# Holding back the second half of two indirect scatters in a mixture-of-experts and scan kernel

## The chip, the cores and the metric

The kernel runs on one core of a Trainium2 chip. The metric is the device time of one execution in microseconds; each kernel is run several times and the median counts. The engines are TensorE (PE, with its weight loads as PEld), VectorE (DVE), ScalarE (ACT), GpSimd (POOL) and SyncE (SP), which only issues DMAs. They run side by side and are tied together by semaphores.

## The reference, cut to what matters

The input is x of 32 x 256 tokens with 128 features. Three blocks follow one another, each on a layer-normed input and added to the residual; the first and the last are the same feed-forward block with the same weights.

```python
def ffn(x, Wr, br, W1, b1, W2, b2):              # 16 experts, 128 -> 256 -> 128
    probs = softmax(x @ Wr + br)
    w, idx = top_k(probs, 2); w = w / sum(w)
    comb = zeros(T, 16).at[arange(T)[:, None], idx].add(w)
    h = gelu(einsum('td,edh->teh', x, W1) + b1)  # exact gelu
    o = einsum('teh,eho->teo', h, W2) + b2
    return x + einsum('teo,te->to', o, comb)

def attn(x, gamma, wq, wk, wv, wa, wg, wo):
    xn = rms_norm(x) * gamma
    q, k, v, a, g = xn @ wq, xn @ wk, xn @ wv, xn @ wa, xn @ wg
    a = complex(*split(a)); a = sigmoid(abs(a)) * exp(1j * angle(a))
    y = real(associative_scan(y[t] = a[t] * y[t-1] + k[t] * v[t]))   # along the sequence
    return (q * y * silu(g)) @ wo

x = x + 0.5 * ffn(layernorm(x)); x = x + attn(layernorm(x)); x = x + 0.5 * ffn(layernorm(x))
```

## The kernel before, in words

The tokens are cut into four groups (g = 0 to 3) of 2048, 16 tiles of 128 tokens each, and every group stays in SBUF as X[:, g]. The feed-forward block is done twice (f = 0 and f = 1). The kernel computes only the chosen experts: the router's result is turned into a row number for each of a token's two choices, the normed rows are scattered to DRAM sorted by expert, the experts run over tiles of 128 sorted rows, and their results are gathered back and added.

One hand-written list, ORDER, gives the order of all steps, and each engine walks it and does its own part of every step. The steps that matter here:

- R(f, g), K(f, g): router logits on TensorE; VectorE picks the two experts, ranks the rows and writes the row numbers IDX (L1039).
- P(f, g): POOL's scatter. Its first half is 16 indirect DMAs of one tile each (L466), for every token's first choice. The second half (L474) is 16 more for the second choice. Before each eight of these POOL waits until eight of the first half have landed and copies the second weight into the rows' last column (L471). Every indirect DMA is issued by POOL and moves 128 rows.
- E(f, g, half, lo, hi): experts over the pairs of tiles from lo to hi. SP loads the sorted rows (xs, L366) and the experts' weights (WUP, L360), four tiles' rows at a time. Before the first rows of a group it waits until that group's scatter has landed. TensorE transposes the rows (L776), multiplies by the up weights (L786) and the down weights (L803); ScalarE moves what lies between out of PSUM (xsT L551, hidT L532, eo L540) and issues the stores to rows_out (L546). A group has 24 pairs. The pairs are counted through the kernel by the semaphore eo_sb.
- G(f, g, lo, hi): POOL's gather (L487), quarters lo to hi of a group, 8 indirect DMAs for a quarter.
- C(f, g, lo, hi): VectorE adds the gathered rows to X (L1069, L1070).
- N, S, T, A0, A, I, H, A1, J, AP, U, A2, A3 (g): the middle block for a group. T: transposes (L837), A0 and A: 24 products on TensorE (L863), counted through the kernel by the semaphore proj_ps (1 to 24 for group 0, 25 to 48 for group 1, 49 to 72 for group 2, 73 to 96 for group 3); then long VectorE operations on 128x2048 tiles, ScalarE's functions and a scan; A3: the output projection (L875, 16 products in four banks), which VectorE adds to X bank by bank (L1139).

The groups are staggered: while the middle block of one group runs its scan, the experts of the one before and the one after it fill TensorE. POOL's own order around the change is P(1,0), G(0,3), P(1,1), G(1,0), P(1,2), G(1,1). On TensorE the order is: last experts of (0,2); A3 of group 1; the last four pairs of (0,3); T and A of group 2; experts 0 to 8 of (1,0); 8 to 20 of (1,0); A3 of group 2; and the same again one group later.

So that POOL's DMAs don't all come at once, each of them can be held back. Two tables give, for every DMA of every P and G step, the number of expert pairs (PAIRS_BY) and of attention products (PRODUCTS_BY) that must have been made:

```python
def keep_behind(st, i):
    if i % 1 == 0 and PAIRS_BY[st][i // 1] > waited[0]:
        waited[0] = PAIRS_BY[st][i // 1]
        pool.wait_ge(eo_sb, waited[0])
    if i % 1 == 0 and PRODUCTS_BY[st][i // 1] > waited[1]:
        waited[1] = PRODUCTS_BY[st][i // 1]
        pool.wait_ge(proj_ps, waited[1])
```

A wait that was made once isn't made again. A P step has 32 entries, the first 16 for its first half. In P(1,0) the pairs' table ends at 95, in P(1,1) at 119.

Of the kernel before, what the change touches and what calls it, by code (L numbers as in the profile page):

```python
# [16 lines left out]
P = 128  # L17
# [86 lines left out]
               ("P", 0, 3, 0): (20, 20, 20, 20, 20, 20, 20, 20, 20, 20, 20, 20, 20, 20, 20, 20, 20, 20, 20, 20, 20, 20, 21, 23, 24, 26, 27, 29, 30, 32, 33, 34),  # L104
               ("G", 0, 2, 0, 3): (36, 38, 39, 41, 42, 44, 44, 44, 44, 44, 44, 44, 44, 44, 44, 44, 44, 44, 44, 44, 44, 44, 44, 44),
               ("G", 0, 2, 3, 4): (44, 44, 44, 44, 44, 44, 44, 44),
               ("P", 1, 0, 0): (44, 44, 44, 44, 44, 44, 44, 44, 44, 44, 44, 44, 44, 44, 44, 44, 44, 44, 44, 44, 44, 44, 44, 44, 44, 44, 44, 44, 44, 44, 46, 47),
               ("G", 0, 3, 0, 2): (49, 50, 52, 53, 55, 56, 58, 59, 61, 62, 63, 65, 66, 68, 68, 68),
               ("G", 0, 3, 2, 3): (68, 68, 68, 68, 68, 68, 68, 68), ("G", 0, 3, 3, 4): (68, 68, 68, 68, 68, 68, 68, 68),
               ("P", 1, 1, 0): (68, 68, 68, 68, 68, 68, 68, 68, 68, 68, 68, 68, 68, 68, 68, 68, 68, 68, 68, 68, 68, 68, 68, 68, 68, 68, 68, 68, 68, 68, 70, 71),  # L110
               ("G", 1, 0, 0, 4): (73, 74, 76, 77, 79, 80, 82, 83, 85, 86, 88, 89, 91, 92, 92, 92, 92, 92, 92, 92, 92, 92, 92, 92, 92, 92, 92, 92, 92, 92, 92, 92),
               ("P", 1, 2, 0): (92, 92, 92, 92, 92, 92, 92, 92, 92, 92, 92, 92, 92, 92, 92, 92, 92, 92, 92, 92, 92, 92, 92, 92, 92, 92, 92, 92, 92, 92, 92, 92),
               ("G", 1, 1, 0, 1): (92, 92, 92, 92, 92, 92, 92, 92), ("G", 1, 1, 1, 2): (92, 92, 92, 92, 92, 92, 92, 92),
# [1077 lines left out]
```

## Time and profile before

| | |
|---|---|
| median of 3 runs | 983.22 us (975.99 to 983.95) |
| span of the profiled execution | 994.3 us |
| TensorE matmul busy | 725.1 us, 73% |
| VectorE busy | 546.3 us, 55% |
| ScalarE busy | 514.7 us, 52% |
| GpSimd busy | 590.6 us, 59% |
| mean granted TensorE clock | 0.858 of full |
| DMA | 167.13 MB, 168 GB/s over the span |

A profiled execution is one execution on the chip, recorded instruction by instruction; its span runs from the first to the last instruction, and all times below count from its start. Busy time is the time in which an engine had an instruction under way; a matmul's end is modelled, so the moment at which another engine gets its result can be later than the recorded end.

### The profile page before, as it was taken

How to read it: one execution, taken by the hardware profiler on the slowest of the kernel's cores; microseconds unless marked ns; L12 is line 12 of the kernel's file. 1: busy time of each engine (PE TensorE's matmuls, PEld its weight loads, DVE VectorE, ACT ScalarE, POOL GpSimd, SP SyncE). 2: the span in 40 equal slices, each digit the busy share in tenths (PEclk: the TensorE clock that was granted, in tenths of full speed). 3: DMA queues.
4: the chain of work that ended last, by engine and by line, in shares of the span. 5: the costliest groups of instructions: out<-in, count | busy, mean ns of one | idle time of the engine just before them, and what ended most of it. 6: DMA issues, size and time to landing. Idle time of an engine off the chain costs nothing.

```text
span 994.3 us, 15862 instructions
## 1 busy us (share of the span) xinstructions
PE 725.1 (73%) x4409; PEld 607.2 (61%) x4410; DVE 546.3 (55%) x1352; ACT 514.7 (52%) x1071; POOL 590.6 (59%) x551
## 2 busy tenths in 40 slices
PE   4775888786876888669777967685968648977761
PEld 4234788685366873469644867534958627777650
DVE  7983103106689955799745996647876455010201
ACT  1111556455777637676277773576664315444340
POOL 2277441555777747758467457378657545655555
PEclk9995899889977989789788779795989759999986
DMA  9995587774146833176441456321758517778863
GB/s 327 299 348 165 149 234 228 208 202 130 40 123 195 224 111 105 42 202 194 121 124 46 129 161 202 99 66 40 217 167 250 141 41 199 221 207 226 234 201 103
DMA packets 188846, 167.13 MB, mean 168 GB/s; under 512 B 18976, under 2 KB 176480, under 8 KB 187744
## 3 DMA queue, kind: packets, MB, share of 16 engines
q1 hardware_dynamic: 120736, 106.83, 36.6%
q0 software_dynamic: 16384, 33.72, 11.5%
q10 hardware_dynamic: 51648, 25.63, 8.8%
q8 instruction: 39, 0.64, 0.3%
q14 instruction: 39, 0.32, 0.1%
HBM read 104.57 MB, written 61.51 MB: 167 GB/s over the span
## 4 chain that ended last, share of the span: by engine, by line
PE 48%; issue 12%; ACT 12%; another core or an unknown queue 9%; SPq 7%; DVE 5%; DMA 5%; ACTq 0%; DVEq 0%
PE bank L786 17%; PE bank L803 16%; PE bank L863 7%; DMA WUP<-up_weights 4%; PE bank L776 4%; ACT eo L540 2%; SPq L319 2%; PE bank L758 2%; SPq L360 1%; SPq L330 1%; ACT hidT L532 1%; PE bank L702 1%; ACT ci L623 1%; ACT xsT L551 1%
## 5 line engine op out<-in xcount | busy, mean ns | idle before, releaser
L487 POOL DMA_INDIRECT got<-rows_out,IDX x256 | 285.8, 1117 | 194.2 <-ACT eo L540 86.5
L786 PE MATMUL bank<-xsT,WUP 128*128 128x128 f32 x1564 | 240.0, 303 | 77.4 <-ACT xsT L551 51.1
L786 PEld LDWEIGHTS bank<-xsT,WUP 128*128 128x128 f32 x1564 | 218.8, 216 | 85.9 <-issue 75.2
L803 PE MATMUL bank<-W,hidT 128*128 x1564 | 221.0, 286 | 41.5 <-ACT hidT L532 32.1
L803 PEld LDWEIGHTS bank<-W,hidT 128*128 128x128 f32 x1564 | 199.3, 199 | 51.4 <-issue 49.6
L466 POOL DMA_INDIRECT rows_in<-XL,IDX x128 | 157.1, 1227 | 109.3 <-DVE IDX L1039 46.5
L474 POOL DMA_INDIRECT rows_in<-XL,IDX x128 | 136.3, 1065 | 91.7 <-ACT eo L540 53.7
L540 ACT ACTIVATE eo<-bank,xs 128x128 f32<-128x128 f32 x391 | 122.7, 367 | 109.9 <-PE bank L803 74.6
L532 ACT ACTIVATE hidT<-bank 128x512 f32<-128x512 f32 x200 | 118.1, 591 | 116.1 <-PE bank L786 72.8
L551 ACT ACTIVATE xsT<-bank 128x256 f32<-128x256 f32 x200 | 74.0, 377 | 86.2 <-remote 39.2
L863 PE MATMUL bank<-XT,WA 128*128 128x512 f32 x192 | 94.6, 654 | 21.2 <-DVE qg L1090 10.4
L776 PE MATMUL bank<-ident,xs 128*128 128x128 f32 x391 | 81.8, 301 | 5.7 <-issue 3.1
L1069 DVE TENSOR_TENSOR X<-got,X 128x512 f32<-128x512 f32 x32 | 22.0, 686 | 116.3 <-DMA got<-rows_out,IDX 102.2
L863 PEld LDWEIGHTS bank<-XT,WA 128*128 128x128 f32 x192 | 39.1, 207 | 72.8 <-issue 57.6
L1062 DVE TENSOR_TENSOR X<-bank,X 128x512 f32<-128x512 f32 x32 | 21.3, 687 | 96.5 <-issue 41.4
L776 PEld LDWEIGHTS bank<-ident,xs 128*128 128x128 f32 x391 | 56.4, 161 | 8.5 <-issue 8.2
L712 PE MATMUL bank<-WR,hidT 128*128 128x16 f32 x192 | 38.9, 341 | 21.9 <-issue 20.9
L712 PEld LDWEIGHTS bank<-WR,hidT 128*128 128x128 f32 x192 | 38.5, 297 | 23.9 <-issue 23.8
L758 PE MATMUL bank<-B,CT 128*128 128x512 f32 x64 | 37.0, 708 | 15.8 <-issue 9.0
L913 DVE BATCH_NORM_STATS2 stats<-X 128x6 f32<-128x128 f32 x192 | 38.3, 278 | 6.0 <-DMA X<-in_L_attn_x 5.8
L1011 DVE TENSOR_SCALAR den<-gexp 128x16 f32<-128x16 f32 x8 | 1.4, 173 | 62.0 <-ACT gexp L516 60.8
L969 DVE TENSOR_SCALAR XL<-X,rs,nb 128x128 f32<-128x128 f32 x128 | 33.8, 360 | 1.0 <-DVE rs L951 0.8
(150 smaller groups left out, 900.4 us busy)
## 6 DMA issues: line engine op xcount, KB each, us to landing
WUP<-up_weights SPq DMA_DIRECT2D x400, 128.0 KB
xs<-rows_in SPq DMA_DIRECT2D x100, 258.0 KB
rows_out<-eo ACTq DMA_DIRECT2D x91, 256.0 KB
rows_in<-kv SPq DMA_DIRECT2D x16, 774.0 KB, 12.1
X<-in_L_attn_x SPq DMA_DIRECT2D x4, 1024.0 KB, 7.7
rows_in<-XL,IDX POOLq DMA_INDIRECT x256
got<-rows_out,IDX POOLq DMA_INDIRECT x256
out<-X SPq DMA_DIRECT2D x4, 1024.0 KB
```

The lines of the kernel that those rows point to most:

```text
L466: pool.indirect_dma_start(rows_in[slot], bass.IndirectOffsetOnAxis(IDX[:, g, j, 0:1], 0), XL[:, b, j, :], None).then_inc(first_put[i], 16)
L474: pool.indirect_dma_start(rows_in[slot], bass.IndirectOffsetOnAxis(IDX[:, g, j, 1:2], 0), XL[:, b, j, :], None).then_inc(scattered[which], 16)
L487: pool.indirect_dma_start(got[:, k, j, :], None, rows_out[SLOT[f, g, half]][0:rows, :], bass.IndirectOffsetOnAxis(IDX[:, g, j, k:k + 1], 0 ...
L532: act.activation(hidT[:, v, 0:tiles * 2 * P], ps[2 + v][:, 0:tiles * 2 * P], ACT.Gelu).then_inc(hid_sb, 1)
L540: ins = act.activation(eo[:, u // 2, t, :], ps[6 + u % 2][:, a * D:(a + 1) * D], ACT.Copy, scale=xs[:, buf, t, D:D + 1])
L551: act.activation(xsT[:, v, 0:tiles * P], ps[v][:, 0:tiles * P], ACT.Copy).then_inc(xsT_sb, 1)
L712: ins = pe.matmul(ps[4][:, j * E:(j + 1) * E], rowsT[i - 1][:, j % 4 * P:(j % 4 + 1) * P], WR[:], start=True, stop=True)
L758: pe.matmul(ps[5 - i][:], CT[:, half * P:(half + 1) * P], B2[:, i, :], start=True, stop=True).then_inc(bias_ps, 1)
L776: ins = pe.transpose(ps[u % 2][:, a * P:(a + 1) * P], xs[:, buf, u % 2 * 2 + a, 0:D], ident[:])
L786: ins = pe.matmul(ps[2 + u % 2][:, k * P:(k + 1) * P], WUP[:, u, a, c * P:(c + 1) * P], xsT[:, u % 2, a * P:(a + 1) * P], start=True, stop ...
L803: ins = pe.matmul(o, hidT[:, v, (2 * a + c) * P:(2 * a + c + 1) * P], W2[:, ds(e * H + c * D, D)], start=(c == 0), stop=(c == 1))
L863: pe.matmul(ps[turns_of[k % 6]][:], WA[:, w, :], XT[:, blk * 512:(blk + 1) * 512], start=True, stop=True).then_inc(proj_ps, 1)
```

## The change

Two rows of PRODUCTS_BY are changed, those of P(1,0) and P(1,1). In each, the second 16 entries are set to the number of the first product of the next group's attention, 49 (group 2) and 73 (group 3). The first 16 entries stay; the two entries of 46 and 47 (70 and 71), which the counts have passed when the scatter starts, go away. Nothing else is changed: the same DMAs in the same order, on the same queue.

```diff
-               ("P", 1, 0, 0): (44, 44, 44, 44, 44, 44, 44, 44, 44, 44, 44, 44, 44, 44, 44, 44, 44, 44, 44, 44, 44, 44, 44, 44, 44, 44, 44, 44, 44, 44, 46, 47),
+               ("P", 1, 0, 0): (44, 44, 44, 44, 44, 44, 44, 44, 44, 44, 44, 44, 44, 44, 44, 44, 49, 49, 49, 49, 49, 49, 49, 49, 49, 49, 49, 49, 49, 49, 49, 49),
                ("G", 0, 3, 0, 2): (49, 50, 52, 53, 55, 56, 58, 59, 61, 62, 63, 65, 66, 68, 68, 68),
                ("G", 0, 3, 2, 3): (68, 68, 68, 68, 68, 68, 68, 68), ("G", 0, 3, 3, 4): (68, 68, 68, 68, 68, 68, 68, 68),
-               ("P", 1, 1, 0): (68, 68, 68, 68, 68, 68, 68, 68, 68, 68, 68, 68, 68, 68, 68, 68, 68, 68, 68, 68, 68, 68, 68, 68, 68, 68, 68, 68, 68, 68, 70, 71),
+               ("P", 1, 1, 0): (68, 68, 68, 68, 68, 68, 68, 68, 68, 68, 68, 68, 68, 68, 68, 68, 73, 73, 73, 73, 73, 73, 73, 73, 73, 73, 73, 73, 73, 73, 73, 73),
                ("G", 1, 0, 0, 4): (73, 74, 76, 77, 79, 80, 82, 83, 85, 86, 88, 89, 91, 92, 92, 92, 92, 92, 92, 92, 92, 92, 92, 92, 92, 92, 92, 92, 92, 92, 92, 92),
```

## Rows read from the trace of the kernel before

**Rows 1.** The page: busy time by engine, and the chain's shares by engine and by line.

```profile
PE 725.1 (73%) x4409; PEld 607.2 (61%) x4410; DVE 546.3 (55%) x1352; ACT 514.7 (52%) x1071; POOL 590.6 (59%) x551
...
PE 48%; issue 12%; ACT 12%; another core or an unknown queue 9%; SPq 7%; DVE 5%; DMA 5%; ACTq 0%; DVEq 0%
...
PE bank L786 17%; PE bank L803 16%; PE bank L863 7%; DMA WUP<-up_weights 4%; PE bank L776 4%; ACT eo L540 2%; SPq L319 2%; PE bank L758 2%; SPq L360 1%; SPq L330 1%; ACT hidT L532 1%; PE bank L702 1%; ACT ci L623 1%; ACT xsT L551 1%
```

**Rows 2.** POOL's timeline around P(1,0)'s second half: start, us, line, output and input, idle before it.

```profile
477.93 0.98 POOL L474 DMA_INDIRECT rows_in<-XL,IDX  x1 [0.28 <-issue]
...
486.79 0.96 POOL L474 DMA_INDIRECT rows_in<-XL,IDX  x1 [0.30 <-issue]
...
507.06 0.96 POOL L474 DMA_INDIRECT rows_in<-XL,IDX  x1 [0.30 <-issue]
...
511.16 0.97 POOL L487 DMA_INDIRECT got<-rows_out,IDX  x1 [3.15 <-PE bank L863]
```

**Rows 3.** POOL's timeline at G(1,0)'s start.

```profile
646.19 0.98 POOL L487 DMA_INDIRECT got<-rows_out,IDX  x1 [5.72 <-PE bank L863]
```

**Rows 4.** SP's timeline, loads of sorted rows; several issues are merged.

```profile
509.46 1.48 SPq L366 DMA_DIRECT2D xs<-rows_in  x3
...
641.86 1.48 SPq L366 DMA_DIRECT2D xs<-rows_in  x3
...
762.61 1.25 SPq L366 DMA_DIRECT2D xs<-rows_in  x2
```

**Rows 5.** The chain in order of time: start, us, what.

```profile
89.36 3.08 DMA xs<-rows_in
...
784.59 16.80 another core or an unknown queue
```

**Rows 6.** TensorE's timeline: output projections and first transposes of rows.

```profile
475.88 7.26 PE L875 MATMUL bank<-WO,kv 128*128 128x128 f32 x32 [0.71 <-issue]
...
550.29 1.09 PE L776 MATMUL bank<-ident,xs 128*128 128x128 f32 x4
...
692.88 1.06 PE L776 MATMUL bank<-ident,xs 128*128 128x128 f32 x4
...
761.15 7.23 PE L875 MATMUL bank<-WO,kv 128*128 128x128 f32 x32 [1.28 <-issue]
...
768.22 0.60 PE L776 MATMUL bank<-ident,xs 128*128 128x128 f32 x4
```

**Rows 7.** VectorE's timeline: last projection bank of groups 1 to 3, additions of gathered rows.

```profile
488.24 0.69 DVE L1139 TENSOR_TENSOR X<-bank,X 128x512 f32<-128x512 f32 x1 [3.55 <-remote]
...
571.08 0.68 DVE L1069 TENSOR_TENSOR X<-got,X 128x512 f32<-128x512 f32 x1
...
622.45 0.69 DVE L1139 TENSOR_TENSOR X<-bank,X 128x512 f32<-128x512 f32 x1 [3.57 <-remote]
...
728.00 0.69 DVE L1069 TENSOR_TENSOR X<-got,X 128x512 f32<-128x512 f32 x1
...
768.42 0.69 DVE L1139 TENSOR_TENSOR X<-bank,X 128x512 f32<-128x512 f32 x1 [1.06 <-issue]
```

**Rows 8.** POOL's timeline in G(0,3) and at P(1,1)'s start.

```profile
542.81 2.57 POOL L487 DMA_INDIRECT got<-rows_out,IDX  x1 [0.30 <-issue]
...
580.19 1.45 POOL L466 DMA_INDIRECT rows_in<-XL,IDX  x1 [11.24 <-DVE IDX L1039]
```

**Rows 9.** POOL's timeline in P(1,2).

```profile
700.45 1.00 POOL L466 DMA_INDIRECT rows_in<-XL,IDX  x1 [3.78 <-ACT eo L540]
...
738.97 1.03 POOL L474 DMA_INDIRECT rows_in<-XL,IDX  x1 [6.06 <-ACT eo L540]
...
744.99 1.42 POOL L474 DMA_INDIRECT rows_in<-XL,IDX  x1 [0.91 <-ACT eo L540]
...
760.23 0.96 POOL L474 DMA_INDIRECT rows_in<-XL,IDX  x1 [0.30 <-issue]
```

**Rows 10.** A stretch: length, busy us of each engine (instructions), granted clock, DMA share, GB/s.

```profile
553.00:580.00 27.00, 18.83 (x146) 18.23 (x146) 25.83 (x49) 20.83 (x39) 7.19 (x6) 0.82 0.62 173
```

## The prediction

> **What bounds the kernel now.** I read the page first: TensorE is the busiest engine and holds nearly half of the chain that ended last, GpSimd (POOL) is busy 59% of the span and has no line of its own in that chain [rows 1]. So POOL costs time only where somebody waits for one of its DMAs. The change moves 2 x 16 of them, so the second view is POOL's timeline around the two scatters, to be read for two things: when the second half (L474) runs today, and what POOL does behind it. In the first scatter, P(1,0), the second half starts at 477.93, straight behind the first half; its last DMA starts at 507.06. Then POOL waits until 511.16, where the product count reaches 49, for the first gather of group 3 [rows 2]. In P(1,1) the pattern is the same: behind its last scatter POOL waits 5.72 us, until 646.19, for count 73 [rows 3]. Third, the readers of what POOL delivers: SP's loads of rows (L366), TensorE's first transposes on them (L776), VectorE's additions of gathered rows (L1069) and the indices that start the next scatter [rows 4 to 8].
>
> **Where the scatters go.** 49 and 73 are the counts for which the first gather behind each scatter waits already. So I take the start from those gathers: the second halves begin at 511.16 and 646.19. Eight undisturbed scatters have their first and last starts 8.86 us apart, 1.266 us each [rows 2]; 16 of them and the weight copies between take 16 x 1.266 + 0.5 = 20.7 us. What is queued behind them on POOL goes back by 20.7 us: 32 gathers of group 3, then P(1,1); 32 gathers of group 0, then P(1,2), then the gathers of group 1. No DMA is added or taken away, and the wait is one that POOL would make a few lines later.
>
> **First site, cover by cover.** (a) SP waits for the scatter before it loads the first rows of the next experts, at 509.46 today, 1.4 us after the last scatter ended (507.06 + 0.96). It would load at 511.16 + 20.7 + 1.4 = 533.3; a load of rows shows 3.08 us in the chain [rows 5], so they are there at 536.4, and TensorE asks at 550.29: 13.9 us of cover [rows 4, 6]. Behind that load SP has only the next rows and the weights of the same stage. Cost 0. (b) The first 16 gathers of group 3 would run from 531.9. Undisturbed, one takes 0.94 + 0.30 = 1.24 us. A gather at 542.81 took 2.57 us, and its next three some 2 us, while VectorE was in operations on whole 128x2048 tiles [rows 8]; with 4.7 us for those four, the 16 are done at 557, plus 2 for landing. VectorE adds them at 571.08 [rows 7]: 12 us of cover. The other 16 end near 580, and their additions come after the next scan, some 30 us behind the first ones. Cost 0. (c) P(1,1) starts at 580.19, when its indices are written, and POOL idled 11.24 us before it [rows 8]. Laid end to end, 32 x 1.24 + 4.7 and 3 more for other held ones from 531.9 give 579.3: just in time. A few us late would not matter, since that scatter's second half now waits till 646 anyway. Cost 0.
>
> A rule bears on the held DMAs. The gather at 542.81 is held beside VectorE operations with two SBUF inputs. The Trainium skill, SBUF — State Buffer, "Who interferes with whom", says that such an operation takes only a read interface and, as an inference, leaves descriptor generation alone. This trace does not agree; by the rule the 4.7 us would be 0 and the second site below would end some 3 us earlier, at a cost of 0. The sum stays with the rows.
>
> **Second site.** (a) SP's load at 641.86 goes to 646.19 + 20.7 + 1.4 and some 2 us for held scatters = 670, rows there at 673; TensorE takes them at 692.88 [rows 4, 6]: 19 us. (b) Gathers of group 0 would run from 669. Before, they ran from 646.19 to 696.67 (700.45 less the wait of 3.78) [rows 3, 9], 50.5 us; with the same holds they end at about 719 and have landed by 721. VectorE adds them from 728.00 [rows 7]: 7 us of cover. (c) P(1,2) started at 700.45 and would start at 719. From here the slack is thin. From 646.19 to its end at 761.19 (760.23 + 0.96) POOL waited for pair counts six times, from the 3.78 us at 700.45 to 0.91 us at 744.99, the longest 6.06 us at 738.97, in all 13.6 us, 11.8 us beyond the 0.3 us that every DMA has anyway [rows 9]. So the end can move by 20.7 - 11.8 = 8.9 us at most if everything else stays, and by 0 at least. Laid out: first 16 to 739.3 (16 x 1.266), four more and the copy to 745, then 12 x 1.266 + 0.5 + four held by 1.06 = 19.9, end 764.9: 3.7 us later. (d) This one has a near reader: SP waited for it and loaded at 762.61; with 3.1 us the rows are there at 765.7, TensorE takes them at 768.22 [rows 4, 6], a slack of 2.5 us. So the cost is 3.7 - 2.5 = 1.2 us, between 0 and 8.9 - 2.5 = 6.4. I count it as on the path in full: the pairs that read these rows stand in TensorE's queue ahead of the last group's router.
>
> **DMA traffic.** In 553 to 580 five gathers ran beside eight pairs of experts at a DMA share of 0.62 [rows 10]; now there would be some 19. Waits for expert weights make 4% of the chain [rows 1], 40 us over 200 pairs, 0.2 us a pair; were they doubled for these eight pairs, that is 1.6 us. Between 0 and 1.6; I take 0.3, since the share is far from full. In 478 to 508 traffic falls, and TensorE's long wait there is not for a DMA. Gain 0.
>
> Sum: +1.2 + 0.3 = +1.5 us on a span of 994.3. The three timed runs lie at 976 to 984, so the profiled execution is some 11 us longer; a term of 1.5 us carries over as it is: 983.2 + 1.5 = 984.7, with 983.2 to 991.2 as this case's own range (0 to 6.4 + 1.6).
>
> **Rival 1, the scatters hold TensorE up today.** After the attention of groups 1 and 2 the output projection's 32 matmuls (L875) are issued in 7.26 us, from 475.88 in group 1 [rows 6], which ends at 483.14, yet VectorE gets the last bank at 488.24, 5.1 us later, after a wait of 3.55 us; in group 2 it waits 3.57 us, until 622.45 [rows 7]. Scatters of exactly the moved half run beside. The same matmuls in group 3, from 761.15 for 7.23 us with gathers beside them, hand over at 768.42, at once [rows 6, 7]. The next norm waits for that bank, so about 5.1 us lie on the path, twice. If the scatters do it, the gain is 10.2 us less the 1.5: 974.5. Against it: group 3's gathers are DMAs of the same queue and do no harm there, and 16.80 us of waiting that the chain can't name stand at 784.59, beside gathers alone [rows 5]. If half of it comes back elsewhere, the gain is 3 to 4 us.
> The Trainium skill, SBUF — State Buffer, "Who interferes with whom", states that TensorE and ScalarE never wait on anyone and that a DMA never contends with a compute engine; by it this rival brings nothing and the time is the forecast's. The late hand-over is then something that the change leaves.
>
> **Rival 2, POOL's backlog reaches the path.** The 20.7 us go into a stretch in which POOL catches up only by its waits. It decides once P(1,2)'s last scatter ends after 761.2 + 2.5 = 763.7. If the pair counts come at the same times, the price is at most 6.4; if more DMAs are held by VectorE (1.06 us each), it nears the full 20.7 - 2.5 = 18.2. The middle of the two and 0.3 for traffic gives 12: 995. For it: POOL is idle little in 664 to 761; against it: 6.06 us of waiting in one piece [rows 9].
>
> **Rival 3, it moves nothing.** The waits could be met already, or the covers take all: 983.2. The rows deny the first (count 49 lets POOL go at 511, not at 478) [rows 2]; the second is the forecast's lower end.
>
> **How the numbers follow.** Forecast case 0.57; rival 1 0.26 (974.5, from 970 to 980); rival 2 0.12 (995); nothing at all 0.05. What a measurement of this kernel can tell from no change is about 1%, 9.8 us: 973.4 and 993.0. Faster by over 1%: 0.20, most of rival 1, whose full size stands on that line and which the runs' own spread of 0.8% can carry over it; slower by over 1%: 0.11, nearly all of rival 2; within 1%: 0.69. Range 972 to 991: the forecast's own, and most of rival 1; rival 2 is left out.
>
> **What would show it.** POOL idle from 477.9 to 511 and from about 610 to 646, the second halves as one run of about 21 us behind the first products; SP's loads near 533 and 670; TensorE's transposes at 550 and 693 unmoved; POOL without its 11 us pause before 580; P(1,2)'s end at 762 to 768, SP's load 1.4 us behind. Rival 1 shows in the last L1139 of groups 1 and 2: right behind L875 if true, still 5 us late if not. I am wrong if these hand-overs close up, if TensorE waits for P(1,2)'s rows by more than 6 us, or if its transposes (L776) wait for rows at 550 or 693.

## The result and the profile after

The changed kernel takes 988.95 us (median of 15 runs, 982.27 to 1006.25), the kernel before 977.99 us beside it (15 runs, 971.54 to 990.59). The ratio is 1.0136, 95% interval 1.0110 to 1.0162: slower by 1.4%, some 13 us. The forecast was +1.5 us.

The two profiled executions don't show this as a total: 992.0 us after, 994.3 us before. Single executions differ by more than the effect, so they have to be read stretch by stretch. The page of the kernel after:

```profile
PE 730.7 (74%) x4409; PEld 607.1 (61%) x4410; DVE 546.3 (55%) x1352; ACT 515.0 (52%) x1071; POOL 600.1 (60%) x551
...
PE 49%; ACT 13%; issue 12%; DVE 8%; another core or an unknown queue 6%; DMA 5%; SPq 4%; POOL 1%; ACTq 0%; POOLq 0%; DVEq 0%
...
L803 PE MATMUL bank<-W,hidT 128*128 x1564 | 225.6, 289 | 46.8 <-issue 30.7
```

POOL has taken hardly anything of the chain (1%), and nothing in the busy times stands out. The row of L803, the down products of the experts, counts 46.8 us in which TensorE was idle just before one of them (41.5 in the kernel before); it matters below. POOL's timeline answers to [rows 2, 3, 9]:

```profile
505.60 0.98 POOL L474 DMA_INDIRECT rows_in<-XL,IDX  x1 [27.08 <-PE bank L863]
...
529.22 0.98 POOL L487 DMA_INDIRECT got<-rows_out,IDX  x1 [0.30 <-issue]
...
580.12 4.57 POOL L466 DMA_INDIRECT rows_in<-XL,IDX  x1 [0.30 <-issue]
...
636.85 0.98 POOL L474 DMA_INDIRECT rows_in<-XL,IDX  x1 [26.88 <-PE bank L863]
...
661.03 0.98 POOL L487 DMA_INDIRECT got<-rows_out,IDX  x1 [0.30 <-issue]
...
713.07 1.00 POOL L466 DMA_INDIRECT rows_in<-XL,IDX  x1 [0.30 <-issue]
...
727.05 0.96 POOL L466 DMA_INDIRECT rows_in<-XL,IDX  x1 [0.30 <-issue]
...
767.13 0.96 POOL L474 DMA_INDIRECT rows_in<-XL,IDX  x1 [0.30 <-issue]
```

The waits do what they say: POOL is idle for 27.08 us until the first product of group 2 and for 26.88 us until that of group 3. The second halves take 23.6 us (505.60 to 529.22) and 24.2 us (636.85 to 661.03). P(1,1) starts straight behind the last gather (580.12, idle 0.30), and from 636.85 to 728.0 POOL has no pause longer than 1.07 us. P(1,2) starts at 713.07 and ends at 767.13 + 0.96 = 768.1. The readers and the marks of TensorE's course, in answer to [rows 4, 6, 7]:

```profile
530.62 1.49 SPq L366 DMA_DIRECT2D xs<-rows_in  x3
...
662.26 1.48 SPq L366 DMA_DIRECT2D xs<-rows_in  x3
...
769.57 1.29 SPq L366 DMA_DIRECT2D xs<-rows_in  x2
```

```profile
479.63 7.26 PE L875 MATMUL bank<-WO,kv 128*128 128x128 f32 x32 [2.53 <-ACT eo L540]
502.79 9.18 PE L863 MATMUL bank<-XT,WA 128*128 128x512 f32 x14 [2.24 <-ACT XT L582]
...
545.47 1.09 PE L776 MATMUL bank<-ident,xs 128*128 128x128 f32 x4
...
611.47 7.25 PE L875 MATMUL bank<-WO,kv 128*128 128x128 f32 x32 [4.68 <-ACT eo L540]
634.52 9.23 PE L863 MATMUL bank<-XT,WA 128*128 128x512 f32 x17 [2.90 <-ACT XT L582]
...
683.74 1.06 PE L776 MATMUL bank<-ident,xs 128*128 128x128 f32 x4
...
768.16 7.23 PE L875 MATMUL bank<-WO,kv 128*128 128x128 f32 x32 [1.29 <-issue]
775.23 0.60 PE L776 MATMUL bank<-ident,xs 128*128 128x128 f32 x4
```

```profile
486.93 0.69 DVE L1139 TENSOR_TENSOR X<-bank,X 128x512 f32<-128x512 f32 x1 [1.06 <-PE bank L875]
...
618.76 0.69 DVE L1139 TENSOR_TENSOR X<-bank,X 128x512 f32<-128x512 f32 x1 [1.06 <-PE bank L875]
```

No transpose (L776) waits for rows: at 545.47, 683.74 and 775.23 there is no idle time ahead of them. And the last bank of the output projection is taken by VectorE (L1139) at 486.93 and 618.76, within 0.1 us of the end of L875 (479.63 + 7.26, 611.47 + 7.25). The late hand-over of 5.1 us in groups 1 and 2 [rows 6, 7] is gone, which was the sign for rival 1. The first product then follows at 502.79 and 634.52. In the kernel before it came later behind the same matmuls:

```profile
508.31 9.43 PE L863 MATMUL bank<-XT,WA 128*128 128x512 f32 x16 [2.88 <-issue]
...
643.33 9.32 PE L863 MATMUL bank<-XT,WA 128*128 128x512 f32 x14 [5.02 <-ACT XT L582]
```

From the end of L875 to the first product of the next group that is 25.2 and 26.0 us before, 15.9 and 15.8 us after: 19.5 us won. They are lost again further on. In the last pairs before the second half of experts (1,1) the trace has TensorE idle for 12.95 us:

```profile
711.50 1.06 PE L786 MATMUL bank<-xsT,WUP 128*128 128x128 f32 x8
714.54 1.15 PE L803 MATMUL bank<-W,hidT 128*128 x8 [1.99 <-issue]
728.65 2.07 PE L803 MATMUL bank<-W,hidT 128*128 x8 [12.95 <-issue]
```

```profile
727.85 0.60 ACT L532 ACTIVATE hidT<-bank 128x512 f32<-128x512 f32 x1 [9.18 <-remote]
```

The trace puts the 12.95 us ahead of the eight matmuls L803 at 728.65 down to "issue", to nothing that it knows, but the order of events says more. These matmuls follow ScalarE's hidT at once (727.85 + 0.60 = 728.45), and ScalarE waited for the last up products, L786, whose recorded end is 711.50 + 1.06 = 712.56: it got them 15.3 us later. Nothing that these up products needed is shown as missing. This is what "stand-still" means below: a result of matmuls already issued reaches the next engine many us late, and TensorE has nothing else to do meanwhile. Whether TensorE works late or only its signal is late, the trace doesn't tell, since matmul ends are modelled. The stand-still lies beside the first twelve scatters of P(1,2), which run without a break from 713.07 to 728.01.

### The profile page after: what moved, and what is told of

The parts are those of the page before. It is cut to its first block, busy times and chain, and to the rows that moved or that the text cites. A ratio compares the mean times of both kernels' runs of the same rounds, so it can differ in the third digit from the quotient of the medians.

```text
span 992.0 us, 15862 instructions
## 1 busy us (share of the span) xinstructions
PE 730.7 (74%) x4409; PEld 607.1 (61%) x4410; DVE 546.3 (55%) x1352; ACT 515.0 (52%) x1071; POOL 600.1 (60%) x551
## 4 chain that ended last, share of the span: by engine, by line
PE 49%; ACT 13%; issue 12%; DVE 8%; another core or an unknown queue 6%; DMA 5%; SPq 4%; POOL 1%; ACTq 0%; POOLq 0%; DVEq 0%
PE bank L786 15%; PE bank L803 13%; PE bank L863 8%; DMA WUP<-up_weights 5%; PE bank L776 4%; PE bank L875 3%; PE bank L712 3%; SPq L360 3%; ACT eo L540 2%; PE bank L758 2%; PE bank L702 2%; ACT hidT L532 1%; ACT kv L502 1%; ACT XT L582 1%
## 5 line engine op out<-in xcount | busy, mean ns | idle before, releaser
L487 POOL DMA_INDIRECT got<-rows_out,IDX x256 | 292.9, 1144 | 159.8 <-issue 74.7
L786 PE MATMUL bank<-xsT,WUP 128*128 128x128 f32 x1564 | 233.4, 297 | 59.8 <-ACT xsT L551 37.6
L803 PE MATMUL bank<-W,hidT 128*128 x1564 | 225.6, 289 | 46.8 <-issue 30.7
L786 PEld LDWEIGHTS bank<-xsT,WUP 128*128 128x128 f32 x1564 | 212.3, 210 | 68.4 <-issue 53.9
L803 PEld LDWEIGHTS bank<-W,hidT 128*128 128x128 f32 x1564 | 201.9, 201 | 60.1 <-issue 57.6
L532 ACT ACTIVATE hidT<-bank 128x512 f32<-128x512 f32 x200 | 118.2, 591 | 117.9 <-PE bank L786 57.3
L863 PE MATMUL bank<-XT,WA 128*128 128x512 f32 x192 | 94.7, 654 | 18.5 <-ACT XT L582 8.0
L776 PE MATMUL bank<-ident,xs 128*128 128x128 f32 x391 | 82.0, 301 | 3.7 <-DMA xs<-rows_in 1.9
L863 PEld LDWEIGHTS bank<-XT,WA 128*128 128x128 f32 x192 | 39.2, 208 | 70.3 <-issue 58.7
L1062 DVE TENSOR_TENSOR X<-bank,X 128x512 f32<-128x512 f32 x32 | 21.3, 687 | 103.8 <-PE bank L758 94.7
L776 PEld LDWEIGHTS bank<-ident,xs 128*128 128x128 f32 x391 | 55.2, 160 | 6.4 <-issue 5.7
L875 PE MATMUL bank<-WO,kv 128*128 128x128 f32 x128 | 29.0, 399 | 14.5 <-issue 7.3
L875 PEld LDWEIGHTS bank<-WO,kv 128*128 128x128 f32 x128 | 28.3, 311 | 15.3 <-issue 7.7
## 6 DMA issues: line engine op xcount, KB each, us to landing
rows_in<-kv SPq DMA_DIRECT2D x16, 774.0 KB, 12.4
```

Source lines behind the costliest of these rows:

```text
L487: pool.indirect_dma_start(got[:, k, j, :], None, rows_out[SLOT[f, g, half]][0:rows, :], bass.IndirectOffsetOnAxis(IDX[:, g, j, k:k + 1], 0 ...
L532: act.activation(hidT[:, v, 0:tiles * 2 * P], ps[2 + v][:, 0:tiles * 2 * P], ACT.Gelu).then_inc(hid_sb, 1)
L776: ins = pe.transpose(ps[u % 2][:, a * P:(a + 1) * P], xs[:, buf, u % 2 * 2 + a, 0:D], ident[:])
L786: ins = pe.matmul(ps[2 + u % 2][:, k * P:(k + 1) * P], WUP[:, u, a, c * P:(c + 1) * P], xsT[:, u % 2, a * P:(a + 1) * P], start=True, stop ...
L803: ins = pe.matmul(o, hidT[:, v, (2 * a + c) * P:(2 * a + c + 1) * P], W2[:, ds(e * H + c * D, D)], start=(c == 0), stop=(c == 1))
L863: pe.matmul(ps[turns_of[k % 6]][:], WA[:, w, :], XT[:, blk * 512:(blk + 1) * 512], start=True, stop=True).then_inc(proj_ps, 1)
```

## Four stretches that can be compared

I cut every execution at the same marks: the ends of the three output projections (start plus duration of L875) and the first product of groups 2 and 3 (first L863 behind it). The runs were made in six series, each on one chip. They are of two kinds, told apart by what the kernel before takes in them: 978 to 997 us in four (called slow chips here, the first result's series among them; the record doesn't name its chip), 880 and 883 us in two (quick chips). None of the five chips that are named was used twice, so that the chip makes the difference, and not the hour, is likely but not shown. "Held" are kernels in which both second halves wait for 49 and 73; kernels in which the second half of P(1,0) or P(1,1) waits for something else are not in the table. "A3(1) to 49" is the passage from the end of group 1's output projection to product 49, and so on; "rest" runs from A3(3) to the end. The time ahead of the first mark is left out.

| us | kernel | A3(1) to 49 | 49 to A3(2) | A3(2) to 73 | 73 to A3(3) | rest |
|---|---|---|---|---|---|---|
| slow | before | 25.2 | 109.0 | 26.0 | 125.0 | 225.9 |
| slow | after | 15.9 | 115.9 | 15.8 | 140.9 | 216.6 |
| slow | after again (h4) | 15.9 | 116.0 | 15.8 | 140.3 | 216.4 |
| slow | before, readers late (g2) | 23.2 | 110.8 | 24.7 | 122.3 | 234.8 |
| slow | after, readers late (g1) | 15.9 | 114.6 | 15.8 | 142.3 | 235.2 |
| slow | before, half gather (h1, k2) | 21.4, 16.7 | 108.3, 107.7 | 23.3, 22.3 | 123.7, 122.8 | 212.8, 216.1 |
| slow | after, half gather (g4, k1) | 15.9, 15.9 | 117.1, 112.6 | 15.7, 15.8 | 121.5, 125.6 | 220.6, 221.2 |
| slow | after, repaced (h3) | 15.9 | 110.6 | 15.8 | 127.3 | 226.2 |
| quick | before (f1) | 15.9 | 107.6 | 15.7 | 120.0 | 176.8 |
| quick | after (f2) | 15.9 | 109.1 | 15.8 | 122.4 | 188.1 |

Each value is from one execution. The last column and the time ahead of the first mark vary from trace to trace without following the change: on slow chips, in the usual order of steps, the rest is 212.8 to 225.9 us where nothing is held and 216.4 to 226.2 where both are. So the columns don't add up to the measured ratios.

The experiments are told in the order in which they were made; S, B and C are the theories named in the expectations.

## Experiments: which site, and by how much

**Only the first site.** The diffs stand against the kernel before unless it is said otherwise, in PRODUCTS_BY unless another table is named; 44 x 16 is sixteen entries of 44.

```diff
-("P", 1, 0, 0): 44 x 30, 46, 47
+("P", 1, 0, 0): 44 x 16, 49 x 16
```

> Only P(1,0)'s second half waits for product 49; P(1,1) is as before. Theory S (the stream: POOL, robbed of its pauses, issues indirect DMAs without a break in the stretch around 712 to 728 of the changed kernel, and TensorE stands still beside it, 15.3 us there): the price belongs to the second site, where POOL is busy from 637 to 728 without a pause; the first site has an 11 us pause before P(1,1) as a buffer, so this kernel takes 978 +-4, a ratio of 0.995 to 1.004. Theory B (a backlog of POOL that delivers rows late, whichever site): the first site's readers have 12 us of cover and more, so also 1.00. Theory C (scatters or gathers beside attention and experts slow them, at each site alike): half of the 1.4%, 985, ratio 1.007.

Measured on a quick chip: 883.62 us against 882.65, ratio 0.9997 (0.9969 to 1.0024). The first site costs nothing there, as the prediction had it.

**Only the second site.**

```diff
-("P", 1, 1, 0): 68 x 30, 70, 71
+("P", 1, 1, 0): 68 x 16, 73 x 16
```

> Only P(1,1)'s second half waits for product 73; P(1,0) is as before. Theory S: nearly all of the loss, 985 to 992, ratio 1.010 to 1.016, with a stall of TensorE by more than 8 us in the twelve pairs of experts (1,1) beside an unbroken stream of POOL. Theory B: the same total, but TensorE waits for rows loaded behind P(1,2) (5 to 7 us near 768), not in the middle of experts (1,1). Theory C: half, 1.007.

896.49 us, ratio 1.0147 (1.0107 to 1.0187): the whole loss, on a chip on which the trace has no stand-still at all. TensorE waits 10.35 us at 717.37, for rows. That is theory B.

**Until the output projection is over.** Pair 93 and pair 117 are the first that TensorE makes behind A3.

In PAIRS_BY of the kernel before, the last sixteen entries:

```diff
-("P", 1, 0, 0): ..., 89, 90, 91, 91, 91, 91, 92, 92, 93, 94, 95 x 6
+("P", 1, 0, 0): ..., 93 x 9, 94, 95 x 6
-("P", 1, 1, 0): ..., 113, 114, 115, 115, 115, 115, 116, 116, 117, 118, 119 x 6
+("P", 1, 1, 0): ..., 117 x 9, 118, 119 x 6
```

> The second halves wait only until the output projection is over: for pair 93 (P(1,0)) and pair 117 (P(1,1)), near 492 and 623, some 14 us earlier than in the changed kernel, 14 us later than before. They end near 513 and 644, where they ended before within 6 us, so POOL keeps its later pauses. Theory S and B both: the loss of the changed kernel goes away, and if the hand-over of the output projection was held up by scatters (5.1 us late in two groups), there is a gain: 968 to 978, ratio 0.99 to 1.00. Theory C: scatters run beside attention as much as in the changed kernel, so it stays 0.5 to 1% slower than before.

885.12 us, ratio 1.0034 (1.0006 to 1.0062): a little over the range that S and B gave.

**P(1,2) without its pair counts.**

In PAIRS_BY of the kernel before:

```diff
-("P", 1, 2, 0): 121, 122, 122, 123, ..., 141, 142
+("P", 1, 2, 0): 120 x 32
```

> The kernel before with no pair count ahead of P(1,2)'s scatters: the scatters run in one stream from some 697 to 738, right behind the gathers of (1,0), and nothing is delivered later than before. Theory S: TensorE stalls beside this stream as in the changed kernel, 5 to 15 us: 983 to 992, ratio 1.005 to 1.015. Theory B: nothing is late, the rows are even earlier: ratio 0.995 to 1.002. Theory C has no more DMAs here than before, but closer together beside experts (1,1): up to 1.003.

882.41 us, ratio 0.9991 (0.9958 to 1.0023). An unbroken stream alone costs nothing on a quick chip. But the stream was not the quick one of some 40 us that I expected: P(1,2) starts at 637.61, once its indices are written, has no pause longer than 0.33 us, and still takes 56.1 us (to 693.76), while with its pair counts it takes 54.8 us in the kernel before on the other quick chip. Taking the waits away gave nothing back.

**Before and after on one quick chip.** Both are unchanged kernels.

> The kernel before, once more, for a trace from the same chip as the kernels beside it. In the runs on the quicker chip (before: 882.65) P(1,2)'s last scatter ended at 698.9 with only the first site changed, and TensorE took its rows at 706.8, right behind the last output projection. Theory B: the same here within 3 us, and no wait of TensorE ahead of those rows. Theory S: here too stand-stills of TensorE in the experts, beside long streams.

> The changed kernel, on the same chip as the others of this series. Theory B (POOL's backlog at the second site delivers P(1,2)'s rows late, the first site costs nothing): the ratio of the kernel with the second site alone, 1.0147 within 0.004, and in the trace P(1,2)'s last scatter some 14 us later than in the kernel before, TensorE's transposes of its rows some 10 us behind the last output projection. Theory S: the loss sits in stand-stills in the middle of experts, 5 us and more each. If both sites cost, more than 1.019.

The kernel after takes 895.34 us against 880.47, ratio 1.0161 (1.0133 to 1.0189). The kernel before, its timelines of TensorE and POOL:

```profile
557.76 7.26 PE L875 MATMUL bank<-WO,kv 128*128 128x128 f32 x32 [0.72 <-ACT eo L540]
580.74 9.23 PE L863 MATMUL bank<-XT,WA 128*128 128x512 f32 x17 [2.89 <-ACT XT L582]
...
693.47 7.23 PE L875 MATMUL bank<-WO,kv 128*128 128x128 f32 x32 [1.29 <-issue]
700.54 0.60 PE L776 MATMUL bank<-ident,xs 128*128 128x128 f32 x4
```

```profile
582.84 0.98 POOL L487 DMA_INDIRECT got<-rows_out,IDX  x1 [2.42 <-PE bank L863]
...
636.51 1.00 POOL L466 DMA_INDIRECT rows_in<-XL,IDX  x1 [4.56 <-ACT eo L540]
...
690.33 0.96 POOL L474 DMA_INDIRECT rows_in<-XL,IDX  x1 [0.30 <-issue]
```

And the kernel after:

```profile
698.24 7.22 PE L875 MATMUL bank<-WO,kv 128*128 128x128 f32 x32 [1.29 <-issue]
715.94 1.09 PE L776 MATMUL bank<-ident,xs 128*128 128x128 f32 x4 [10.47 <-DMA xs<-rows_in]
```

```profile
585.86 0.98 POOL L474 DMA_INDIRECT rows_in<-XL,IDX  x1 [18.69 <-PE bank L863]
...
609.09 0.97 POOL L487 DMA_INDIRECT got<-rows_out,IDX  x1 [0.31 <-issue]
...
660.82 1.00 POOL L466 DMA_INDIRECT rows_in<-XL,IDX  x1 [0.31 <-issue]
...
710.55 0.96 POOL L474 DMA_INDIRECT rows_in<-XL,IDX  x1 [0.30 <-issue]
```

The last row of TensorE is the price: the first transposes of P(1,2)'s rows wait 10.47 us for "DMA xs<-rows_in"; before they followed the output projection at once. From POOL's first DMA behind product 73 to the end of P(1,2) it is 108.5 us before (582.84 to 691.29) and 125.7 after (585.86 to 711.51), 17.2 us more. Of the second half's 23.2 us the gathers with the pause behind them (4.56 us at 636.51) gave back 1.9, since they ran slower than before, and P(1,2) itself 4.1 (54.8 us before, 50.7 after). Nothing else gave.

**Router first.** One edit of the changed kernel's order: R(1,3) ahead of the four pairs that read those rows.

```diff
-("A3", 3), ("E", 1, 2, 0, 0, 4), ("N", (1, 3), None), ("R", 1, 3), ("B", 1, 2, 0), ("K", 1, 3, 0),
+("A3", 3), ("N", (1, 3), None), ("R", 1, 3), ("E", 1, 2, 0, 0, 4), ("B", 1, 2, 0), ("K", 1, 3, 0),
```

> The changed kernel with the last group's norm and router, R(1,3), ahead of the four pairs of experts E(1,2,0,0,4) that read P(1,2)'s rows. The scatters come as late as before, but their first reader stands where TensorE would otherwise wait for the picks K(1,3). Theory B: the price goes away but for 0 to 3 us: ratio to before 0.998 to 1.004. Theory S, or contention of DMAs: the reader's place doesn't matter, and it stays at 1.012 to 1.017.

903.42 us, ratio 1.0235 (1.0201 to 1.0268): a miss, worse than the change itself. A reading of the order and the trace: the picks K(1,3) need a bias step on TensorE and an exponential on ScalarE, and both now stood behind the late pairs: VectorE's L1062 came at 738.95. The order had more readers than the one I moved, so this run doesn't judge theory B.

**Only the last eight.**

```diff
-("P", 1, 1, 0): 68 x 30, 70, 71
+("P", 1, 1, 0): 68 x 24, 73 x 8
```

> Only the last eight scatters of P(1,1) wait for product 73. They were held behind pair 117 already, some 15 us short of that. Theory B: the backlog is 10.4 us in place of 20.7, less the few us that they ran past the output projection before; the cushion ahead of TensorE is 3.4 us, so 2 to 6 us remain: ratio 1.002 to 1.007. Were the price set by whether anything is queued behind product 73, and not by how much, it would be as with all sixteen, 1.0147.

886.14 us, ratio 1.0057 (1.0035 to 1.0079), in the range of B. With it the quick chips give a row of doses. The third column is the end of P(1,2) less the end of L875 in group 3, the fourth TensorE's idle time ahead of L776:

| kernel | ratio | end of P(1,2) | wait |
|---|---|---|---|
| before (f1) | | -9.4 | none |
| first site only (e1) | 0.9997 | -8.1 | none |
| pairs 93 and 117 (e3) | 1.0034 | -3.3 | 1.08 |
| last eight (f4) | 1.0057 | -2.1 | 2.22 |
| second site only (e2) | 1.0147 | +6.0 | 10.35 |
| after (f2) | 1.0161 | +6.1 | 10.47 |

In all four that wait, it is the third column plus 4.3 to 4.4 us, the way from the last scatter over SP's load to the transpose. The cushion in the kernel before is 9.4 - 4.4 = 5 us. The wait is most of the loss: 10.5 of 14.2 us for the kernel after.

## Experiments: what else happens on a slow chip

**The readers late, after and before.** The four pairs stand behind all of K(1,3), once in the kernel after and once in the kernel before.

```diff
-("E", 1, 2, 0, 0, 4), ("N", (1, 3), None), ("R", 1, 3), ("B", 1, 2, 0), ("K", 1, 3, 0), ("K", 1, 3, 1),
+("N", (1, 3), None), ("R", 1, 3), ("B", 1, 2, 0), ("K", 1, 3, 0), ("K", 1, 3, 1), ("E", 1, 2, 0, 0, 4),
```

> The changed kernel with the four pairs E(1,2,0,0,4), the first readers of P(1,2)'s rows, behind the last group's norm, router and picks. Theory B: rows that come 10 us late are then early, since nobody asks for them before the picks; what remains is the price of the order itself, TensorE idle for 8.8 us during the norm: a ratio to before of 1.003 to 1.012, and the same time as the kernel before in this order (next kernel) within 0.4%. If something other than the lateness of these rows costs, the two differ by about 1.4% as the kernels themselves do.

> The kernel before in the same order, the control. Theory B: 1.003 to 1.012 of before, since the four pairs no longer fill TensorE's wait for the norm; the kernel above within 0.4% of it.

These fell on a slow chip (before: 995.75 us): ratio 1.0222 (1.0164 to 1.0281) after, 1.0154 (1.0102 to 1.0206) before. The order costs more than I gave it, and the difference of 0.7% lies between the two answers, the intervals overlapping. Inconclusive as a test of B; but the traces say why it had to be: on a slow chip A3(3) itself is late in the kernel after (142.3 us against 122.3), so the rows are not what is late.

**Held to product 85.** Against the kernel after:

```diff
-("P", 1, 1, 0): 68 x 16, 73 x 16
+("P", 1, 1, 0): 68 x 16, 85 x 16
```

> The changed kernel with P(1,1)'s second half held to product 85 in place of 73, 13 us later still; its own first reader has some 19 us left after the change and so stays covered. Theory B, with POOL full from the second half to the end of P(1,2): every us of delay goes through, P(1,2)'s last scatter comes 13 us later again, and the loss is 14 + 13 = 27 us: ratio 1.026 to 1.034. If POOL still had pauses to give, or the price were of another kind, it would stay at 1.015 to 1.02.

1016.25 us, ratio 1.0183 (1.0121 to 1.0245), less than expected and on a slow chip, on which the kernel after was not run as it is. The stretch from 73 to A3(3) is 153.9 us, 13 more than in the kernel after, so the delay went through there, with TensorE idle for 18.31 and 6.21 us ahead of the last two groups of L803 in that half of experts (735.36 and 743.64), the place of the stand-still above; the total is short of it by an amount that this run doesn't explain.

**Half a gather.** Against the kernel after, and for its control against the kernel before. The 16 gathers of group 0's second choice are left out, so its last addition uses old rows.

```diff
                     for k in range(2):
                         keep_behind(("G", f, g, lo, hi), 2 * j - lo * T // 2 + k)
+                        if (f, g, k) == (1, 0, 1):
+                            continue
...
-                    dve.wait_ge(got_in[q], 16 * 8 * (n + 1))
+                    dve.wait_ge(got_in[q], 16 * 8 * (n + 1) - (64 if n > 3 else 0))
```

> The changed kernel with both waits as they are, but G(1,0) gathers only each token's first choice; the 16 gathers of the second choice are left out, so group 0's last addition is of old rows. That takes some 16 x 1.3 = 21 us of work out of POOL's queue between the held scatters and P(1,2). Theory B: P(1,2) ends as early as before or earlier, and the loss goes: ratio 0.996 to 1.003. If the place of the held scatters costs (beside attention and experts) and not what is queued behind them, 1.010 to 1.016 stays.

981.95 us, ratio 0.9833 (0.9789 to 0.9878). Not only was the loss gone, the kernel was 1.7% faster than before, outside of what either theory gave. The next runs ask whether that was the hand-overs or the gathers.

> The control of the kernel with half of G(1,0): the kernel before, with the 16 gathers of group 0's second choice left out. Theory B alone: P(1,2) was early by some 3 to 5 us already, so 0.995 to 1.000, and the changed kernel without these gathers can be no better; that it was, 0.983 on a slow chip, then needs the late hand-overs of the output projection, which the held scatters take away (theory S: some 5 us twice). If this control is at 0.985 too, the gain came from the gathers left out.

978.06 us against 980.08, ratio 0.9987 (0.9951 to 1.0022), on another slow chip. Then both on one chip:

> The changed kernel with the 16 gathers of group 0's second choice left out, once more, now on the same chip as its control. Theory S, on a slow chip (kernel before above 970 us): the hand-overs of both output projections are prompt and POOL has its pauses back, so the kernel is 8 to 16 us faster than the control: 0.984 to 0.992 of before. Theory B alone, and on a quick chip (880 us): no backlog, nothing to win, 0.996 to 1.003, the same as the control within 0.4%.

> The control: the kernel before with the same 16 gathers left out. Measured once at 0.9987; again 0.995 to 1.002 on any chip. Were it below 0.99, leaving gathers out would itself be what made the other kernel faster.

Before: 997.44 us. With half a gather the changed kernel takes 983.60 us, ratio 0.9873 (0.9818 to 0.9929), the kernel before 996.96 us, ratio 0.9989 (0.9953 to 1.0026). So on a slow chip the same two waits are worth 1.2% of gain once POOL has the time for them, a gain known from the timed runs: the stretches of this one pair of traces don't show it (269.9 and 269.5 us over the first four), for k2 lost time ahead of the first mark. TensorE's timeline in the held one, k1 (here L877 is the output projection, L865 the products):

```profile
611.56 7.26 PE L877 MATMUL bank<-WO,kv 128*128 128x128 f32 x32 [0.72 <-ACT eo L542]
634.60 9.23 PE L865 MATMUL bank<-XT,WA 128*128 128x512 f32 x17 [2.88 <-ACT XT L584]
```

And in its control, k2:

```profile
624.34 7.26 PE L877 MATMUL bank<-WO,kv 128*128 128x128 f32 x32 [0.71 <-ACT eo L542]
653.91 9.23 PE L865 MATMUL bank<-XT,WA 128*128 128x512 f32 x17 [2.89 <-issue]
```

611.56 + 7.26 to 634.60 is 15.8 us; 624.34 + 7.26 to 653.91 is 22.3 us. At the first site k2's passage is only 16.7 us, but there TensorE was idle for 6.91 us ahead of the projection itself (499.91), beside the same scatters, and the first mark lies behind that.

**Pairs 93 and 117, on a slow chip.**

> The second halves wait for pair 93 and pair 117 only, once more, for a chip on which TensorE stands still beside streams of scatters. Theory S, on such a chip: the hand-overs after the output projection close up, 10 us less, and POOL is late by a few us only: ratio 0.985 to 0.998. On a chip without stand-stills 1.000 to 1.006, as measured there (1.0034).

986.99 us, ratio 1.0072 (1.0036 to 1.0109), where 0.985 to 0.998 was expected: a miss. The passages did close up (15.9 and 15.8 us), but the two stretches behind them took 118.2 and 133.4 us. The last four of group 2's products came only at 536.41, 32 us behind the first (25 us in the kernel after). SP's loads of rows and weights (516.35 to 522.80) now lie beside the products; whether they are the reason was not tried.

**Repaced.** Against the kernel after, in PAIRS_BY, the first entries; from the 21st on nothing changes:

```diff
-("P", 1, 2, 0): (121, 122, 122, 123, 124, 125, 126, 126, 127, 128, ...
+("P", 1, 2, 0): (129, 129, 130, 130, 131, 131, 132, 132, 132, 132, ...
```

> The changed kernel, with P(1,2)'s scatters tied to the pairs of experts that TensorE is making just then: two each behind pairs 129, 130, 131 and 132, the rest behind 132 at least. POOL then pauses as soon as TensorE falls behind. Theory S, on a chip with stand-stills: the one of 15 to 18 us in that stretch shrinks to 5 or less, and the ratio falls from 1.013 to 0.998 to 1.008, though the scatters end no earlier. Theory B: the pauses only delay POOL further: 1.013 to 1.02. On a chip without stand-stills the pairs are made before the scatters start and nothing changes, 1.014 to 1.017.

> The changed kernel beside the three above, on the same chip: 1.011 to 1.017, whichever chip it is. On a slow one with a stand-still of TensorE by 10 us or more in the first scatters of P(1,2), and prompt hand-overs after both output projections; on a quick one with P(1,2)'s rows late by 10 us.

984.24 us, ratio 1.0061 (1.0027 to 1.0094), and 987.40 us, ratio 1.0068 (1.0032 to 1.0104), on one slow chip. The kernel after shows its stand-still again, at the same eight matmuls and beside the same scatters:

```profile
724.70 2.07 PE L803 MATMUL bank<-W,hidT 128*128 x8 [10.17 <-issue]
```

In the repaced kernel it is absent, 73 to A3(3) took 127.3 us and not 140.3, but another came right behind. VectorE takes the last bank of A3(3), whose matmuls were issued from 745.99 for 7.23 us, only here:

```profile
767.21 0.69 DVE L1139 TENSOR_TENSOR X<-bank,X 128x512 f32<-128x512 f32 x1 [10.57 <-remote]
```

```profile
753.10 0.97 POOL L487 DMA_INDIRECT got<-rows_out,IDX  x1 [0.30 <-issue]
...
763.14 0.94 POOL L487 DMA_INDIRECT got<-rows_out,IDX  x1 [0.30 <-issue]
```

That is 14 us late, beside nine gathers in one stream from 753.10 to 764.08. Ahead of that, P(1,2) ended only 0.4 us before A3(3) and TensorE waited 3.90 us for its rows (at 757.13), the wait known from the quick chips. The net is nothing, 1.0061 against 1.0068. The edit was not the clean test that I meant: when the first scatter came, at 704.16, TensorE had only 16 down products of these pairs left (704.30 and 705.75), so it had hardly any experts in that stretch to stand still in, and no later scatter had to pause.

## Why the prediction was wrong, step by step

**What held.** The sign of the forecast, and that partly by luck: on the slow chips, where it was measured first, the loss is what is left of two larger effects, neither of which is in its sum. The waits act where I put them. At the first site SP loads at 530.62 (533.3 forecast), the transposes at 545.47 don't wait, P(1,1) starts just in time (580.12), and the site alone costs nothing on a quick chip. The additions of gathered rows had their cover.

**The step that failed: the end of P(1,2), +3.7 us.** I let POOL win back 17 of 20.7 us, 11.8 of them from its waits. Measured from its first DMA behind product 73 to the end of P(1,2): 115.0 us before and 131.2 after in the first pair of traces, 108.5 and 125.7 on a quick chip, so 16.2 and 17.2 us more. Three sizes were off. The second half took 23.2 to 24.2 us and not 20.7. P(1,2) took 50.7 (quick) or 55.0 us (slow) and not 45.9: on the quick chip without any waits, so its 32 scatters take 1.58 us each and not the 1.27 of undisturbed ones. And the waits were not slack to be had: with none of them P(1,2) took 56.1 us on a quick chip. The trace of the kernel before could have told: P(1,2) runs there from 700.45 to 761.19, and less the 8.3 us that its five waits for pair counts after the start last beyond 0.3 us each, that is 52.4 us. It has held DMAs, as the 2.57 us in [rows 8] is one; I priced four of them, at 1.06 us each.

**What it meant.** On the quick chips this is rival 2 as it stood: it decides once P(1,2) ends beyond the cushion, and its forecast was +12 us; measured 14.2, of which 10.5 are TensorE's wait for those rows. I gave it 0.12. "The end can move by 8.9 us at most" was the bound that ruled it out, and it was a sum of pauses, no bound.

**On the slow chips**, the result's own among them, nobody waits for those rows (only in the repaced kernel TensorE does, for 3.90 us): P(1,2) ends 7.2 us ahead of A3(3) before and 7.3 after, because the backlog went along with an A3(3) that is itself late. That path to the loss stands in no rival. And rival 1 was right as well (0.26), so the two pull against each other. The passage from A3 to the next product, behind groups 1 and 2, takes 15.7 to 15.9 us in every held trace on any chip and in every trace on a quick chip; on slow chips, with scatters beside the output projection, 16.7 to 26.0 us in eight passages, 22.9 on average. That is a gain of 7 us a passage, 14 in all. Against it stand 5.5 us in the stretch from 49 to A3(2) (114.5 on average in the five kernels with both waits and all gathers, 115.4 us in that held to 85 among them; 109.0 in the four not held) and 17.5 us from 73 to A3(3) (141.2 in three held, 123.7 in two not held). The sum is +9 us; measured +13 on the first chip, +7 on another. With half a gather the 17.5 go down to 0.3 and the sum to about -8; measured -12 (0.9873 less 0.9989, of 997). These sums are rough: they leave out the rest, where the held kernels with half a gather take 6 us more than their controls and the kernel after 9 us less than the one before. That the 17.5 us need the 16 gathers in POOL's queue is shown by four held and four not held traces, and by the ratios of the last pair. That they come by way of the stand-still is read from the traces, and there it is plain. Ahead of the last two groups of eight down products of experts 0 to 12 of (1,1), TensorE is idle for 14.9 us in the kernel after, 12.4 in h4, 16.4 with the readers late (g1) and 24.5 held to 85 (g3), where the stretch takes 17.2, 16.6, 18.6 and 30.2 us more than 123.7. In the other eight traces of slow chips, and in before and after on a quick one, it is at most 0.9 us. Up to 6 us of each stretch lie elsewhere.

**The term for DMA traffic**, +0.3 us, lies in the stretch from 49 to A3(2). It took 1.5 us more on the quick chip (109.1 and 107.6, one trace each) and 5.5 on slow chips. No run singles traffic out.

**Rival 3** was wrong: 49 and 73 moved everything they should.

**What stays open.** What makes TensorE stand still; what the 5.5 us of the first site are on a slow chip, since that site was tried alone on a quick one only; why pairs 93 and 117 lose on a slow chip what they gain. No version with the whole computation beat the kernel before by more than its interval. On a slow chip the gain of 1.2% is there for a kernel that takes 20 us out of POOL's queue between 637 and 713; no kernel here does so and still computes everything.

## What to carry to other kernels

The waiting time of an engine is not slack until it is shown that the instructions behind the wait run at their undisturbed speed: a count that looks late hides how slow they are. Follow a delayed queue to the first reader with a cushion smaller than the delay, and take the delay undiminished as the high end of the range. When a step is held away from a place where it hurts, ask what the queue does in the place where it now runs, and measure on more than one chip before believing a few tenths of a per cent.

## What was not expected of the hardware

The same program differs by 11 to 13% from one series, and chip, to another. The kernel before took 880.47 and 882.65 us in two and 977.99 to 997.44 us in four. The page shows where: idle time ahead of the down products, 46.8 us in the kernel after on a slow chip, above, and in its run on a quick one:

```profile
L803 PE MATMUL bank<-W,hidT 128*128 x1564 | 212.7, 279 | 3.5 <-ACT eo L540 1.2
```

On slow chips TensorE is idle for 5 to 18 us at a time with nothing missing that the trace knows. Three windows of the kernel after, with busy time and count of PE, PEld, DVE, ACT and POOL, then TensorE's granted clock, DMA share and GB/s:

```profile
705.00:712.00 7.00, 6.82 (x61) 6.63 (x61) 3.04 (x4) 4.06 (x12) 5.47 (x6) 1.00 0.87 247
712.00:728.00 16.00, 1.71 (x13) 1.33 (x12) 0.00 (x0) 1.56 (x5) 12.35 (x13) 0.65 0.44 133
728.00:731.00 3.00, 2.35 (x9) 2.21 (x10) 0.00 (x0) 0.71 (x2) 0.01 (x1) 0.50 0.68 180
```

The clock is full until the stand-still, 0.65 in it on average and 0.50, the lower of the two levels (1.2 GHz), behind it, where eight matmuls L803 took 2.07 us and not 1.15. In slices of 2 us it is still 1.00 at 714 to 716, 0.73 in the next and 0.50 from 718 on: it fell while TensorE was idle, so it follows the stand-still and doesn't make it. Between 350 and 900 us the twelve traces of slow chips have fifteen places where TensorE is idle for 5 us or more down to "issue". All fifteen lie beside indirect DMAs that GpSimd issues with no pause longer than 0.5 us, though such streams fill only 59 to 73% of that time; the eight traces of quick chips have no such place, with streams in 85 to 88%. Several end within 2 us of the first pause: the hand-over at 488.24 [rows 7] 0.5 us behind the eighth scatter (486.79 + 0.96) [rows 2]. On quick chips the same streams do nothing: the passage takes 15.7 us beside scatters too. The Trainium skill, SBUF — State Buffer, "Who interferes with whom", lets TensorE wait on nobody and a DMA contend with no compute engine; the quick chips agree (15.7 us with scatters beside and without), the slow chips don't (22.9 and 15.8 us). That is a coincidence in time in every case; no run takes all the DMAs away, and what the slow chips have that the quick ones lack is not known.

What holds a scatter shows in P(1,2) of the kernel after on a quick chip, where POOL has no waits. POOL's rows, then VectorE's at the same times:

```profile
668.54 2.95 POOL L466 DMA_INDIRECT rows_in<-XL,IDX  x1 [0.30 <-issue]
...
677.00 1.44 POOL L466 DMA_INDIRECT rows_in<-XL,IDX  x1 [0.30 <-issue]
```

```profile
668.37 2.29 DVE L1121 SCALAR_TENSOR_TENSOR XT<-ci,kv 128x2048 f32<-128x2048 f32 x1 [0.18 <-ACT ci L626]
...
677.59 4.74 DVE L1127 TENSOR_TENSOR_SCAN S<-S 128x256 f32<-128x256 f32 x8
```

An issue that takes 0.96 us undisturbed takes 2.95 beside an operation on two SBUF inputs of 2048 elements, and 1.44 beside the scan's steps, which run for 9.4 us (one issue beside them, at 674.01, took 0.96); every one above 1.3 us in this step lies beside one of the two. The Trainium skill, the same section, would leave descriptor generation alone beside such an operation; these rows speak against it, though no run took the operations away.
